# Attention steps handed on head by head: exponentials of 512 columns, and attention values between the two heads of a step

## The reference

```python
x = x + attention_0(layernorm(x), ctx_1024, ctx_1024, mask)   # 16 heads of 8 columns
x = x + experts_0(layernorm(x))                               # 32 experts, 8 chosen, and a shared one
x = x + attention_1(layernorm(x), ctx_1024, ctx_1024)         # 16 heads, rotary positions
x = x + experts_1(layernorm(x))                               # 8 experts, 1 chosen, and a shared one
...
logits = einsum('bhqd,bhkd->bhqk', q, k) * scale              # 256 x 512 for each batch and head
out = einsum('bhqk,bhkd->bhqd', softmax(logits), v)
```

## Time and profile before

| what | value |
|---|---|
| median of 3 runs | 779.77 us (779.35 to 785.31) |
| the profiled execution | 783.57 us, of which the span is 782.3 us |
| TensorE busy | 661.6 us (85%) |
| VectorE busy | 529.5 us (68%) |
| ScalarE busy | 407.7 us (52%) |
| GpSimd busy | 378.6 us (48%) |
| mean granted TensorE clock | 0.942 of full speed |

### The profile page before, as it was taken

The page is one execution under the profiler, slowest core; times in us unless marked ns, Lnnn a source line. Parts: engine busy times, 40 slices in busy tenths (PEclk is TensorE's granted clock), DMA queues, the critical chain, the costliest instruction groups (busy, mean ns, idle before and its releaser), DMA issues.

```text
span 782.3 us, 13823 instructions
## 1 busy us (share of the span) xinstructions
PE 661.6 (85%) x5180; PEld 335.3 (43%) x5180; DVE 529.5 (68%) x922; ACT 407.7 (52%) x550; POOL 378.6 (48%) x559
## 2 busy tenths in 40 slices
PE   4378898989888998999999888888898889686992
PEld 2023333333233666666656333333233224345981
DVE  4487888898987566545555588888888853662332
ACT  2037777777675633332222466766766685532441
POOL 6243556665330356687545547557555111180333
PEclk9559999999996999999999999999999999987996
DMA  6865423542302363756723053374394200013004
GB/s 178 176 222 140 119 80 82 139 120 81 67 2 59 75 165 107 175 139 170 172 81 81 0 138 93 101 192 113 93 205 106 99 3 1 8 41 85 28 28 132
DMA packets 57711, 80.07 MB, mean 102 GB/s; under 512 B 6234, under 2 KB 41834, under 8 KB 55402
## 3 DMA queue, kind: packets, MB, share of 16 engines
q1 hardware_dynamic: 56122, 76.42, 38.0%
q0 software_dynamic: 1248, 2.57, 1.0%
q10 hardware_dynamic: 276, 0.21, 0.1%
HBM read 55.86 MB, written 24.29 MB: 102 GB/s over the span
## 4 chain that ended last, share of the span: by engine, by line
PE 48%; ACT 18%; issue 13%; DVE 10%; DMA 5%; SPq 3%; POOL 3%; DVEq 0%; ACTq 0%; POOLq 0%
ACT prob L808 16%; PE pair L425 10%; PE outs L536 6%; PE pair L305 4%; PE pair L307 4%; PE outs L438 4%; PE pair L306 4%; PE pair L393 3%; PE misc L438 3%; PE misc L351 2%; POOL rows_in L1667 2%; PE outs L334 2%; DVE negmax L1082 2%; PE misc L449 1%; DMA x<-in_x 1%
## 5 line engine op out<-in xcount | busy, mean ns | idle before, releaser
L1082 DVE TENSOR_REDUCE negmax<-pair 128x2 f32<-128x1024 f32 x256 | 307.4, 1215 | 58.8 <-PE pair L393 56.0
L808 ACT ACTIVATE prob<-pair 128x1024 f32<-128x1024 f32 x256 | 260.4, 1025 | 117.6 <-PE pair L425 116.8
L425 PE MATMUL pair<-qstack,kstack 54*128 54x256 bf16 x1024 | 103.0, 280 | 43.9 <-ACT prob L808 42.5
L393 PE MATMUL pair<-kstack,qstack 51*128 51x512 bf16 (+1 forms) x512 | 103.0, 399 | 14.2 <-DVE negmax L1082 7.5
L425 PEld LDWEIGHTS pair<-qstack,kstack 54*128 54x128 bf16 x1024 | 29.8, 95 | 162.5 <-ACT prob L808 124.4
L1288 DVE TENSOR_TENSOR hid<-pair,silu 128x512 f32<-128x512 f32 x68 | 46.7, 688 | 74.2 <-PE pair L307 62.1
L914 ACT ACTIVATE silu<-pair 128x512 f32<-128x512 f32 x68 | 40.6, 599 | 92.9 <-PE pair L307 92.5
L438 PE MATMUL outs<-prob,vaug 128*32 128x256 f32 x1024 | 87.0, 405 | 0.0
L438 PE MATMUL misc<-prob,vaug 128*32 128x256 f32 x1024 | 81.0, 391 | 0.2
L305 PE MATMUL pair<-xT,eh 128*128 128x512 f32 x136 | 71.8, 528 | 0.0
L536 PE MATMUL outs<-hid,down 128*128 128x512 f32 x136 | 69.5, 593 | 0.7 <-POOL hid L1621 0.7
(11 more groups left out here) (259 smaller groups left out, 1063.9 us busy)
## 6 DMA issues: line engine op xcount, KB each, us to landing
kstack<-k_terms SPq DMA_DIRECT2D x32, 384.0 KB
w_here<-w_rows SPq DMA_DIRECT2D x32, 256.0 KB, 4.7
w_there<-w_rows SPq DMA_DIRECT2D x32, 256.0 KB, 4.8
k_terms<-kparts SPq DMA_DIRECT2D x16, 384.0 KB, 2.6
qstack<-q_terms SPq DMA_DIRECT2D x32, 192.0 KB, 3.3
ctx_nat<-in_ctxT SPq DMA_DIRECT2D x16, 256.0 KB, 3.5
k_terms<-kparts SPq DMA_DIRECT2D x16, 256.0 KB, 2.9
w_nat<-in_L_gu SPq DMA_DIRECT2D x3, 1056.0 KB, 5.9
```

Of the source, the lines that this page charges most:

```text
L393: return nc.tensor.matmul(to, qstack[n % 3][rows, g, qt * P:(qt + 1) * P], kstack[n % 3][rows, g, :], start=True, stop=True)
L425: e = nc.tensor.matmul(bank[m + r][:, k * SQ:(k + 1) * SQ], kstack[n % 3][rows, g, (c + k) * P:(c + k + 1) * P], qstack[n % 3][rows, g, :] ...
L808: nc.scalar.activation(prob[:, quad % 2, 2 * g:2 * g + 2, c:c + 2, :].rearrange("p j c q -> p j (c q)"), pair[t_pair(n, step)][:, :, :], A ...
L1082: nc.vector.tensor_reduce(negmax[:, n % 2, 2 * g:2 * g + 2, qt], pair[score_pair(n, step)][:, :, :], AX.X, ALU.max, negate=True).then_inc( ...
```

## The change

Each step is cut into its two heads. The transposed scores of one head (two matmuls) get the score matmul of the *other* head's rows between them. The attention values move between the two heads, the rest of the step behind both. The exponential becomes two activations of 512 columns with a semaphore step each. The last period of a layer keeps its exponentials of 1024 columns, but its transposed scores now come as both matmuls of head 0 and then both of head 1, and its values stand ahead of the rest of the step. `s_done` is still counted once in a step, by the score of head 0, which is now the second. The other lines turn counts of `t_done` and `exp_done` to the new numbering.

```diff
-            def score(n, step):
+            def score(n, step, r):
                 m = 2 * score_pair(n, step)
                 stacks_in(n)
-                bank_free(m)
-                bank_free(m + 1)
-                head_scores(bank[m], n, step, 0)
-                head_scores(bank[m + 1], n, step, 1).then_inc(s_done, 1)
-                left[m] = left[m + 1] = max_done, STEPS * n + step + 1
+                bank_free(m + r)
+                e = head_scores(bank[m + r], n, step, r)
+                if r == 0:
+                    e.then_inc(s_done, 1)
+                    left[m] = left[m + 1] = max_done, STEPS * n + step + 1
...
-            def score_transposed(n, step):
+            def score_transposed(n, step, r):
...
                 bank_free(m)
-                bank_free(m + 1)
                 for k in range(2):
-                    for r in range(2):
-                        rows = slice(HALF * r, HALF * r + STACK)
-                        e = nc.tensor.matmul(bank[m + r][:, k * SQ:(k + 1) * SQ], kstack[n % 3][rows, g, (c + k) * P:(c + k + 1) * P],
-                                             qstack[n % 3][rows, g, :], start=True, stop=True)
+                    e = nc.tensor.matmul(bank[m][:, k * SQ:(k + 1) * SQ], kstack[n % 3][rows, g, (c + k) * P:(c + k + 1) * P],
+                                         qstack[n % 3][rows, g, :], start=True, stop=True)
+                    if k == 0 and n % B + 1 < B:
+                        score(n + 1, step, 1 - r)
                 e.then_inc(t_done, 1)
-                left[m] = left[m + 1] = exp_done, STEPS * n + step + 1
+                left[m] = exp_done, exponentials(n, step, r)
...
                     if b >= 0:
-                        score_transposed(n, step)
-                    if b + 1 < B:
-                        score(n + 1, step)
+                        score_transposed(n, step, 0)
+                    if b == B - 1:
+                        score_transposed(n, step, 1)
+                    if b >= 1 and step < 3:
+                        values(n - 1, 3, step + 1)
+                    if b >= 0 and step >= 3:
+                        values(n, (step - 3) // 4, (step - 3) % 4)
+                    if 0 <= b < B - 1:
+                        score_transposed(n, step, 1)
+                    if b < 0:
+                        score(n + 1, step, 1)
+                        score(n + 1, step, 0)
...
-                    if b >= 1 and step < 3:
-                        values(n - 1, 3, step + 1)
-                    if b >= 0 and step >= 3:
-                        values(n, (step - 3) // 4, (step - 3) % 4)
...
             def exponential(n, step):
                 quad, g, c = step // 4, step % 2, step % 4 // 2 * 2
-                act.wait_ge(t_done, STEPS * n + step + 1)
                 act.wait_ge(pv_done, KC * (4 * n + quad - 1))
...
+                else:
+                    for r in range(2):
+                        act.wait_ge(t_done, 2 * (STEPS * n + step) + r + 1)
+                        nc.scalar.activation(prob[:, quad % 2, 2 * g + r, c:c + 2, :].rearrange("p c q -> p (c q)"),
+                                             pair[t_pair(n, step)][:, r, :], ACT.Exp).then_inc(exp_done, 1)
```

More of the change, by code:

```diff
@@ L97, in t_pair, with exponentials @@
     return 1 if n % B == B - 1 and step % 2 else TPAIR
+def exponentials(n, step, r):
+    done = 2 * STEPS * n - STEPS * (n // B)
+    return done + step + 1 if n % B == B - 1 else done + 2 * step + r + 1
 def outputs(half):
@@ L413, in max_turn @@
                 left[m] = mT_copied, 2 * n + half + 1
-            def score_transposed(n, step):
+            def score_transposed(n, step, r):
                 quad, g, c = step // 4, 2 * (step // 4) + step % 2, step % 4 // 2 * 2
-                m = 2 * t_pair(n, step)
+                m, rows = 2 * t_pair(n, step) + r, slice(HALF * r, HALF * r + STACK)
                 pe.wait_ge(ld_m[quad // 2], 32 * (n + 1))
                 bank_free(m)
-                bank_free(m + 1)
                 for k in range(2):
-                    for r in range(2):
-                        rows = slice(HALF * r, HALF * r + STACK)
-                        e = nc.tensor.matmul(bank[m + r][:, k * SQ:(k + 1) * SQ], kstack[n % 3][rows, g, (c + k) * P:(c + k + 1) * P],
-                                             qstack[n % 3][rows, g, :], start=True, stop=True)
+                    e = nc.tensor.matmul(bank[m][:, k * SQ:(k + 1) * SQ], kstack[n % 3][rows, g, (c + k) * P:(c + k + 1) * P],
+                                         qstack[n % 3][rows, g, :], start=True, stop=True)
+                    if k == 0 and n % B + 1 < B:
+                        score(n + 1, step, 1 - r)
                 e.then_inc(t_done, 1)
-                left[m] = left[m + 1] = exp_done, STEPS * n + step + 1
+                left[m] = exp_done, exponentials(n, step, r)
             def values(n, quad, c):
-                pe.wait_ge(exp_done, STEPS * n + 4 * quad + 2 * (c // 2) + 2)
+                pe.wait_ge(exp_done, exponentials(n, 4 * quad + 2 * (c // 2) + 1, 1))
                 pe.wait_ge(v_set, n + 1)
@@ L601, in ffn_0 @@
                     if 36 <= m and m % 2 == 0:
-                        score(B, (m - 36) // 2)
+                        score(B, (m - 36) // 2, 1)
+                        score(B, (m - 36) // 2, 0)
                     if m == 42:
@@ L805, in exponential @@
                 quad, g, c = step // 4, step % 2, step % 4 // 2 * 2
-                act.wait_ge(t_done, STEPS * n + step + 1)
                 act.wait_ge(pv_done, KC * (4 * n + quad - 1))
-                nc.scalar.activation(prob[:, quad % 2, 2 * g:2 * g + 2, c:c + 2, :].rearrange("p j c q -> p j (c q)"),
-                                     pair[t_pair(n, step)][:, :, :], ACT.Exp).then_inc(exp_done, 1)
+                if n % B == B - 1:
+                    act.wait_ge(t_done, 2 * (STEPS * n + step) + 2)
+                    nc.scalar.activation(prob[:, quad % 2, 2 * g:2 * g + 2, c:c + 2, :].rearrange("p j c q -> p j (c q)"),
+                                         pair[t_pair(n, step)][:, :, :], ACT.Exp).then_inc(exp_done, 1)
+                else:
[3 more added lines that the diff above has]
+                                             pair[t_pair(n, step)][:, r, :], ACT.Exp).then_inc(exp_done, 1)
             def split_y(n, m=M):
@@ L957, in ffn_1 @@
                 act.wait_ge(ld_ffn, 224)
-                act.wait_ge(t_done, STEPS * n)
+                act.wait_ge(t_done, 2 * STEPS * n)
                 act.wait_ge(logits_done, NB)
@@ L1394, in ffn_1 @@
                 n = LAYERS * B - 1
-                ve.wait_ge(t_done, STEPS * n)
+                ve.wait_ge(t_done, 2 * STEPS * n)
                 ve.wait_ge(rt_hi, 2)
@@ L1752, in stack_q @@
                 i = n % 3
-                sp.wait_ge(t_done, STEPS * (n - 2))
+                sp.wait_ge(t_done, 2 * STEPS * (n - 2))
                 sp.wait_ge(q_out, 48 * (n + 1))
```

2 lines of the change are left out of this document (1 added, 1 removed).

## The result

| | before | changed |
|---|---|---|
| median | 781.4 us (11 runs) | 789.77 us (11 runs) |
| profiled execution, span | 782.3 us | 790.3 us |

The ratio is 1.0092, with a 95% interval from 1.0075 to 1.0109: 0.9% slower, 8.4 us between the medians. The forecast was +5.4 us.

A forecast was written before the change was run, and what follows sets the result against it. Order of the work, no engine full: a closed loop of 1.51 to 1.52 us a step between transposed scores and exponential. Terms +2.0, +2.5, -1.3, -0.2 and +2.4 gave +5.4 us: 789.0 profiled, 785.2 us median, range 764 to 804.

The forecast's parts named there:

- The loop that is removed: Transposed scores and exponential, 1.51 to 1.52 us a step: head 0's return path becomes 1.08 us and no longer binds.
- the split's price: ScalarE's exponential in two halves: 0.98 to 1.18 us together instead of 1.02, adding 1 to 3 us a period.
- One sign that I named: In the profile after, ScalarE's wait for transposed scores, 0.49 us in each free step, falls by more than half.
- TensorE in the new order: TensorE's step: free 1.12 us instead of 1.11, with a projection 1.85 instead of 1.75, with a turn 1.58.
- VectorE in the new order: Maximum starts 1.33 us into the step, not 0.66; slack to later scores falls from 1.32 to -0.35 us.
- the walk: One full period of layer 0, step by step: 1.05 us lost, 0.65 won, 0.4 us longer in 25.8.
- The sum: All periods and layers added: +5.4 us on the execution, 785.2 us for the median.
- First and seventh periods: Both layers' first periods -1.3 us together, with little on VectorE; seventh periods -0.1 us each, -0.2.
- The last periods: Last period of each layer: three lengths of 256 columns behind one another where there were two, +2.4 us.
- something that would make it wrong: Sign against the prediction: the change moves GpSimd's work or a DMA into a wait absent from the trace of before.
- the first: Faster rival: VectorE keeps up and maxima hold nothing up, -14.5 us, so 765 us; chance 0.22.
- the second: Slower rival: a head's second matmul waits for the score or its weights, +31 us, so 811 us; chance 0.15.

The follow-up runs named there:

- the added operation: One more VectorE memset of 512 scratch columns at step 11 in 12 periods: kernel before, ratio 1.001; changed kernel, ratio 1.0144.
- the moved values: Changed kernel with attention values back behind both heads and the rest of the step, exponentials still split: 781.65 us, ratio 0.9971 to the kernel before.
- the query terms first: Query terms written ahead of the key stack's load in the sync queue: changed kernel 779.91 us, ratio 0.9968; kernel before 780.35 us, ratio 0.9962.

## Why the prediction was right, and where not

*The loop that is removed, and the split's price.* Right in the main. TensorE's transposed scores, before and after, with the idle time ahead of them behind the bar:

```profile
L425 PE MATMUL pair<-qstack,kstack 54*128 54x256 bf16 x1024 | 103.0, 280 | 43.9 <-ACT prob L808 42.5
L429 PE MATMUL pair<-qstack,kstack 54*128 54x256 bf16 x1024 | 191.4, 281 | 5.2 <-ACT prob L826 1.7
```

So 42.5 us of TensorE's idle time ended with an exponential before, and 1.7 us do now. It hasn't gone everywhere: at step 13 of a full period head 0 starts 0.26 us late for it, as shown above, and step 8 takes 1.25 us, not 1.1. A half takes 0.596 us on average. One sign that I named didn't come: ScalarE's wait for transposed scores, 116.8 us before in all, is 90.6 now, a fifth less and not half.

*TensorE in the new order.* Right. The values start 0.32 us behind the transposed scores of head 0 (149.84 to 150.16), head 1 follows at 0.89 (150.73), and a step with a projection takes 1.85 to 1.86 us.

*VectorE in the new order, and the walk.* Right, and shown by the added operation (at step 13) and for the larger part by the moved values, not only argued. For a full period of layer 0 (159.27 on):

| steps | walk, us | measured, us |
|---|---|---|
| 0, 1 | 3.73 | 3.80 |
| 2 to 5 | 6.2 | 6.18 |
| 6, 7 | 3.8 | 3.71 |
| 8, 9 | 2.98 | 3.11 |
| 10 to 13 | 6.60 | 6.56 |
| 14, 15 | 2.78 | 2.86 |

The walk adds up to 26.09 here, 0.33 more than the 25.76 us of before and not 0.4, mostly because I read 3.02 us for steps 14 and 15 of the kernel before and they take 3.11.

Within the group of steps 10 to 13 the split is not as I said: step 13 takes 2.13 us, not 2.7, and steps 10 to 12 take 4.4 instead of 3.9. The values of step 11 now stand ahead of head 1, and wait for a bank until ScalarE has copied the turned maxima of step 10:

```profile
152.09 0.64 PE L444 MATMUL misc<-prob,vaug 128*32 128x256 f32 x8 [0.44 <-ACT mT L814]
```

That wait is paid for by the later one, since the maximum of step 11 decides when step 13 goes on.

*The sum.* Full periods came out at +0.46 in layer 0 (the fifth period, 26.22 against 25.76; +0.4 said) and +0.50 in layer 1 (+0.5 said); with the query terms first in both kernels it is +0.5 in both. The last full period of each layer is an exception that I didn't see, at +0.05 and +0.08: it has no turn of x at step 13, where the turn stands behind VectorE's wait and so counts in full, and that step takes 1.67 instead of 2.13 us. First and seventh periods won more than the 1.5 us said: 4.0 and 1.3. Of the 4.0, 1.25 is the low clock in the profile of before; the seventh periods too have step 13 without the turn. The last periods were mis-sized. I said +2.4 for two matmuls in one half of the rows and then two in the other, and the step is 0.90 us against 0.89: TensorE starts the four as it did, two side by side, one of each head.

```profile
644.33 0.40 PE L429 MATMUL pair<-qstack,kstack 54*128 54x256 bf16 x4
644.65 0.64 PE L444 MATMUL misc<-prob,vaug 128*32 128x256 f32 x8
```

All four are over in 0.40 us (0.39 in the earlier trace rows), where by my estimate three lengths one behind the other would be about 0.5, another 0.12 us. The records of the two matmuls that count `t_done`, the second ones of each head, are the last two, 0.12 us behind the first two (644.45 against 644.33): head 1's first matmul started ahead of head 0's second, which is written before it. The last period of layer 1 is still 0.8 us longer, nearly all of it at step 0 (1.62 against 0.90 us), where its scores wait for the exponential of the last head before it.

*What the sum lacked.* The term that it didn't have is the largest one: the second periods cost +9.5 us where the sum had 0.9, from a DMA chain with 0.6 and 0.9 us of slack that the shorter first periods use up. The prediction named such a wait only as something that would make it wrong, and by this sign it was wrong in part: where 0.05 to 0.2 us were lost to it in three periods of before, TensorE now stands idle for 2.3 and 1.6 us in two others. The total came near because errors offset each other: 8.6 us too little in the second periods, against 3.8 us more won in first and seventh periods, about 2 us less lost in the last ones with all that stands behind them, and 0.8 us by which the first period began earlier. So the walk of a full period was right by its mechanism, and that the total lies within 3 us of the forecast is luck.

*The rivals.* VectorE did hold the scores up (0.28 us of idle time at step 13, and 0.79 with the added operation), so the first is out. Matmuls of 256 and 512 columns do run side by side in the two halves of the rows, so the second is out, as the weight loads in the earlier trace rows had said. The Trainium skill's page "TensorE: Matmul & The Clock Gate", part 3, in its list of what overlaps, lets a weight load overlap a running matmul only in another row group. The weight load of the second matmul of a half runs from 153.79 to 153.89, while the first one, started at 153.78, still runs in the same half; that disagrees, and the measurement decides.

## What to carry to other kernels

When a loop between two engines is cut, ask for every consumer of what was moved: here a reduction that reads both halves waits for the later half, and putting other work between the halves delayed it by 0.67 us a step, which gave back what the cut had won; moved behind both halves, the same work left a gain of 1.7%. Set the time at which each transfer lands beside the time at which it is asked for, before making the stage ahead of it shorter: a slack of 0.6 to 0.9 us was in no busy share, and its loss cost 8.4 us with the lower clock behind it. A rest of a step that may wait for others belongs behind both halves, not between them.

## What was not expected of the hardware

- A matmul of 256 columns in one half of the rows, one of 512 in the other, then a second of 256 in the first: the second starts 0.12 us behind the first (149.84, 149.84, 149.96), and all are followed by work on the whole array at 0.32 us, as with equal lengths.
- Four matmuls written as two for one half of the rows and then two for the other take 0.40 us, like four written by turns (0.39). They don't start in the written order: the third starts beside the first, 0.12 us ahead of the second.
- TensorE's granted clock was 1.00 in whole periods of the kernel before in which it stood idle for 1.2 us at once (step 6 in layer 1). Behind idle time of 2.3 us it was 0.50, that is 1.2 GHz, for 6.8 us (78.09 to 84.90), and a projection added 1.15 us instead of 0.64.
